# Rotary embedding in the second attention stage: rotating chunks of even and odd dimensions on VectorE instead of with a permuting matmul

## The chip, the cores and the metric

The kernel runs on one core of a Trainium2 chip. The metric is the device time of one execution in microseconds (us); lower is better. A program is compared with another by the median of several runs, and each kernel has one profiled execution besides.

## The reference

The reference chains four layers over 8 batches of 512 tokens of 256 values: causal attention with 16 heads and post-norm, a mixture of 7 experts, a second attention with rotary embedding and sigmoid weights, and a second mixture with 8 experts and a last norm. What is changed is in the second attention. Per batch, and per head of 16 dimensions:

```
q = rms_norm(x) @ q_w.T + q_b          # the same for k
x1, x2 = q[..., ::2], q[..., 1::2]     # even and odd dimensions
q_rot = stack([-x2, x1], -1).reshape(q.shape)
q = q * cos + q_rot * sin              # the same for k
scores = q @ k.T / 4
weights = sigmoid(scores) / (sum(sigmoid(scores)) + 1e-8)
```

The tables are `cos(emb)` and `sin(emb)` with `emb = [freqs, freqs]`, so the value of dimension d depends on d and the position.

## The kernel before

**Stages.** a is the first attention, b its experts, c the second attention, d its experts in blocks of 128 rows, e the last norm. Each engine (SP queues DMAs, PE, ACT, DVE, POOL) runs its own unrolled program, and semaphores tie them together.

**Passes of stage c.** `slots` emits a sequence of turns. Turn s projects batch s (transposes of x, then the q, k, v matmuls and the rotation), runs attention for batch s-1 and the output product, norm and routing for batch s-2. I call such a turn a pass. The first pass with a projection (s = 0) has no attention; seven passes (s = 1 to 7) have both. Of these s = 1 ("second") has no routing yet, s = 2 to 6 are the five "body" passes, and s = 7 ("seventh") is the last with a rotation and has no norm of a next batch. All work but attention is a list `others`, dealt out between the attention's steps by fixed weights (`COST`), so that every engine meets the steps in one order written out at build time (`spread_out`, L194).

**The attention's steps.** "st" is a unit of four score matmuls (L706) into one of two ST buffers, "av" the four matmuls with v (L724) into OT. ACT turns scores to weights (L839) in a ring of four. A unit of ST waits until the activation two units back is done. "oe" is ACT's copy of OT (L844), "on" the transpose on PE (L734) and the division on DVE (L909 to L916, which ends in `o_nat`), "oT" and "y" the output product (L742, L750), "rT" and "lg" the transposes and matmuls of the router (L760, L767).

**The projection and rotation of a chunk.** A chunk is 128 rows (16 dimensions of 8 heads) by 512 positions. Chunks 0 and 1 are q, chunks 2 and 3 are k, each for heads 0 to 7 and 8 to 15; the order is 0, 2, 1, 3. Step "qk": PE multiplies (L1462) into one of three shared PSUM banks, ACT adds the bias and copies to one of two `qk_flat` tiles (L1497), for which it waits until the rotation before last has used the tile. Step "ro": PE multiplies the copy by the constant matrix `rot` (L1468), which swaps even and odd rows and changes the sign, into another shared bank. DVE multiplies the copy by the cosines (L1586) and the bank by the sines (L1589), adds (L1594), and splits the sum in a bfloat16 part, a second (L1596 to L1598) and, on POOL, a third (L1629). SP saves the three parts of the chunk to DRAM in one DMA (L1414). Step "st_q", after the second and the fourth chunk: nine DMAs (L608, L612 in `stack_up`) read the parts back in the stacked order that the score matmuls use.

```
L245 project = [("qk", 0), ("qk", 2), ("ro", 0), ("qk", 1), ("ro", 2), ("st_q", 0), ("qk", 3), ("ro", 1),
L246            ("v", 0), ("ro", 3), ("v", 1), ("st_q", 1)]
```

**The banks.** `Banks` gives the three shared PSUM banks out in turn to the keys of `bank_keys` (L289). PE waits, before it writes a bank, until the reader of the use three before is done. In a body pass of stage c there are 24 uses, four of them by "ro".

**Other parts that the change touches.** POOL adds the output bias to x (L1635, `x_res`), once in a pass, after DVE's last row of `x_out` (L943). At the start ACT's queue loads the constants, `rot`, `cos_t` and `sin_t` last (L2050); DVE waits for all of them before its first instruction (L1050), and its first work on the first batch is L1074. The weights of stage c are scaled on DVE by four instructions (L1568). Stage d has row buffers `b_rows`, stage d's tables `t_...` and stage e's statistics in tiles of their own; `carve` takes others from the arena.

## Time and profile before

| what | value |
|---|---|
| runs of the kernel before | 1757.6, 1755.45, 1753.68 us |
| median | 1755.45 us |
| the profiled execution's own time | 1758.4 us |
| its span, from first to last instruction | 1756.7 us |
| PE busy | 1462.9 us, 83% |
| PE weight loads | 954.2 us, 54% |
| DVE busy | 926.7 us, 53% |
| ACT busy | 692.1 us, 39% |
| POOL busy | 494.1 us, 28% |
| mean granted TensorE clock | 0.893 |

In the profile "L12" is line 12 of the kernel. A row of a timeline has the start and the length of an instruction in us, its engine, line, operation, the tile it writes and those it reads, and in brackets how long its engine sat idle before it and what ended that. "x4" means four such instructions merged. A float32 matmul appears as two instructions. Names of tiles are those of the program: `scratch` is `qk_cos`, `mask` is `qk_sin` in stage c. "remote" and "unknown queue" are releases that the profile can't name. A stretch table has the busy time of each engine in a stretch of time.

### The profile page before, as it was taken

How to read it: one execution, taken by the hardware profiler on the slowest of the kernel's cores; microseconds unless marked ns; L12 is line 12 of the kernel's file. 1: busy time of each engine (PE TensorE's matmuls, PEld its weight loads, DVE VectorE, ACT ScalarE, POOL GpSimd, SP SyncE). 2: the span in 40 equal slices, each digit the busy share in tenths (PEclk: the TensorE clock that was granted, in tenths of full speed). 3: DMA queues.
4: the chain of work that ended last, by engine and by line, in shares of the span. 5: the costliest groups of instructions: out<-in, count | busy, mean ns of one | idle time of the engine just before them, and what ended most of it. 6: DMA issues, size and time to landing. Idle time of an engine off the chain costs nothing.

```text
span 1756.7 us, 31255 instructions
## 1 busy us (share of the span) xinstructions
PE 1462.9 (83%) x10303; PEld 954.2 (54%) x10304; DVE 926.7 (53%) x3456; ACT 692.1 (39%) x952; POOL 494.1 (28%) x415
## 2 busy tenths in 40 slices
PE   3688898888988828999848999999998839999992
PEld 1245454454544525666524555555555528999991
DVE  2667758777678431111164667657655353444444
ACT  1154443534434511111016566667665712222223
POOL 4022324243332521121210022321322132444442
PEclk8798888888987858999968999999999959999996
DMA  6854335254350303343134564356427243444446
GB/s 157 199 114 98 80 89 131 70 134 88 78 112 14 110 16 108 99 115 102 22 72 84 121 122 106 82 117 133 101 63 165 77 158 77 72 72 68 73 64 206
DMA packets 119182, 174.27 MB, mean 99 GB/s; under 512 B 17127, under 2 KB 101249, under 8 KB 112912
## 3 DMA queue, kind: packets, MB, share of 16 engines
q1 hardware_dynamic: 95808, 148.05, 34.4%
q0 software_dynamic: 20400, 22.37, 8.0%
q10 hardware_dynamic: 2848, 2.24, 0.4%
q8 instruction: 71, 1.16, 0.3%
q14 instruction: 55, 0.45, 0.1%
HBM read 107.18 MB, written 72.69 MB: 102 GB/s over the span
## 4 chain that ended last, share of the span: by engine, by line
PE 62%; DVE 13%; issue 7%; ACT 4%; DMA 3%; another core or an unknown queue 2%; POOL 1%; SPq 0%; DVEq 0%; POOLq 0%; ACTq 0%
PE ST L706 9%; PE OT L724 8%; PE ST L1813 7%; PE shared L1825 6%; PE ST L1264 6%; DVE scratch L1098 4%; PE OT L1272 3%; PE shared L1272 3%; PE shared L750 3%; PE shared L1462 2%; PE shared L767 2%; PE shared L798 2%; ACT arena L839 2%; PE shared L815 2%
## 5 line engine op out<-in xcount | busy, mean ns | idle before, releaser
L839 ACT ACTIVATE arena<-ST 128x1024 f32<-128x1024 f32 x416 | 414.7, 1024 | 283.8 <-PE ST L706 263.8
L1098 DVE CUSTOM_DVE_ANT_0 scratch<-shared,mask 128x512 bf16<-128x512 f32 (+3 forms) x512 | 229.1, 485 | 90.7 <-PE shared L815 73.7
L706 PE MATMUL ST<-arena 96*128 96x256 bf16 (+2 forms) x1792 | 256.0, 279 | 20.6 <-DMA arena<-qk_parts 13.5
L724 PE MATMUL OT<-arena,v_aug 128*32 128x256 f32 (+1 forms) x3584 | 255.6, 387 | 4.6 <-POOL arena L1166 2.6
L706 PEld LDWEIGHTS ST<-arena 96*128 96x128 bf16 (+1 forms) x1792 | 158.8, 102 | 123.9 <-issue 49.8
L815 PE MATMUL shared<-arena 96*128 96x512 bf16 (+3 forms) x512 | 126.8, 325 | 58.1 <-DVE mx L1098 22.6
L1920 POOL DMA_INDIRECT sum<-arena,block_to_row x71 | 111.0, 1564 | 166.8 <-DMA sum<-arena,block_to_row 115.0
L724 PEld LDWEIGHTS OT<-arena,v_aug 128*32 128x32 f32 x3584 | 85.6, 111 | 120.3 <-issue 74.1
L1166 POOL TENSOR_SCALAR_AFFINE_SELECT arena<-arena 128x512 f32<-128x512 f32 (+1 forms) x96 | 78.6, 819 | 256.6 <-ACT arena L839 256.6
L1825 PE MATMUL shared<-arena 128*128 x568 | 134.2, 379 | 0.0
L815 PEld LDWEIGHTS shared<-arena 96*128 96x128 bf16 x512 | 42.9, 103 | 139.1 <-issue 59.4
L1644 POOL DMA_INDIRECT slot_x<-x_out,row_to x64 | 63.6, 994 | 173.8 <-DVE keep L1557 156.7
L1825 PEld LDWEIGHTS shared<-arena 128*128 128x128 f32 x568 | 102.5, 190 | 11.0
L1629 POOL TENSOR_TENSOR qk_src<-qk_rest,qk_src 128x512 bf16<-128x512 f32 x32 | 38.4, 1201 | 248.5 <-DVE qk_src L1598 248.5
L1264 PE MATMUL ST<-arena 128*128 128x512 f32 x224 | 99.9, 605 | 5.1 <-ACT arena L1283 5.1
L1327 POOL DMA_INDIRECT sum<-arena,b_to x28 | 43.4, 1551 | 179.7 <-DVE arena L1310 171.3
L798 PE MATMUL shared<-xT,w_qkv 128*128 128x512 f32 x128 | 74.7, 718 | 17.3 <-DMA xT<-in_xT 14.8
L1889 DVE COPY arena<-shared 128x256 f32<-128x256 f32 x71 | 30.1, 424 | 97.6 <-PE shared L1803 72.8
L926 DVE TENSOR_TENSOR y_b<-shared,x_res 128x512 f32<-128x512 f32 x32 | 22.1, 691 | 109.5 <-issue 40.3
L1293 DVE TENSOR_SCALAR arena<-ST 128x512 f32<-128x512 f32 x28 | 19.4, 691 | 111.6 <-PE ST L1264 111.6
L1176 POOL DMA_INDIRECT slot_x<-x_out,row_to x64 | 62.6, 979 | 49.6 <-DVE row_to L975 31.8
L1870 ACT ACTIVATE arena<-ST 128x512 f32<-128x512 f32 x70 | 41.8, 597 | 85.0 <-PE ST L1813 80.3
(208 smaller groups left out, 2339.7 us busy)
## 6 DMA issues: line engine op xcount, KB each, us to landing
arena<-qk_parts SPq DMA_DIRECT2D x224, 128.0 KB, 7.1
qk_parts<-qk_src SPq DMA_DIRECT2D x64, 384.0 KB, 2.7
arena<-qk_parts SPq DMA_DIRECT2D x32, 384.0 KB, 4.4
block_rows<-slot_x SPq DMA_DIRECT2D x71, 130.0 KB
arena<-qk_parts SPq DMA_DIRECT2D x32, 256.0 KB, 5.3
sum<-x_out SPq DMA_DIRECT2D x16, 512.0 KB, 2.9
arena<-in_experts_inter SPq DMA_DIRECT2D x7, 1024.0 KB, 5.1
arena<-in_experts_out SPq DMA_DIRECT2D x7, 1024.0 KB, 9.5
```

The lines of the kernel that those rows point to most:

```text
L706: mm = pe.matmul(ST[n % 2][:, i * 256 + at:i * 256 + at + nq], K[par][0:rows, h, kb * P:(kb + 1) * P], Q[par][0:rows, h, q0:q0 + nq], star ...
L724: mm = pe.matmul(OT[32 * i:32 * i + 32, q0:q0 + nq], v_aug[par][:, kb, g * GH + i, :], PT[n % RING][:, i, at:at + nq], start=(u == 0), sto ...
L798: mm = pe.matmul(bank[:, :], w_qkv[:, c, n * P:(n + 1) * P], xT[:, c, :], start=(c == 0), stop=(c == CD - 1))
L815: mm = pe.matmul(bank[:, at:at + S - qb * P], Q[par][0:SK, head, qb * P:(qb + 1) * P], K[par][0:SK, head, qb * P:S], start=True, stop=True)
L839: act.activation(PT[n % RING][:, :, :], ST[n % 2][:, :].rearrange("p (h n) -> p h n", h=GH), func, scale=ATT_SCALE).then_inc(L["exp"], 1)
L1098: taken = dve.tensor_tensor_reduce(out=junk[n % 2][:, at:at + m], in0=bank[:, at:at + m], in1=mask[:, 0:m], scale=1.0, scalar=LOW, op0=ALU ...
L1166: pool.affine_select(out=v, in_=v, compare_op=ALU.is_ge, fill=0.0, base=0, pattern=[[0, GH], [0, blocks], [-1, P]], channel_multiplier=1). ...
L1264: mm = pe.matmul(up_banks[m % 4], wi[par][:, c, m * P:(m + 1) * P], xgT[:, c, :], start=(c == 0), stop=(c == CD - 1))
L1272: mm = pe.matmul(down_banks[t // 2][:, (t % 2) * D:(t % 2 + 1) * D], hT[:, m, t * P:(t + 1) * P], wo[par][:, m, :], start=(m == 0), stop=( ...
L1813: mm = pe.matmul(UP[par][:, f * P:(f + 1) * P], w1_now[par][:, c * F1 + f * P:c * F1 + (f + 1) * P], bxT[par][:, c * P:(c + 1) * P], start ...
L1825: mm = pe.matmul(Y_BANK[par][:, 0:D], bhT[par][:, c * P:(c + 1) * P], w2t[:, bass.ds(e * 1024 + c * D, D)], start=(c == 0), stop=(c == KF ...
L1920: pool.indirect_dma_start(out=sum1, out_offset=bass.IndirectOffsetOnAxis(ap=b_to_row[:, i:i + 1], axis=0), in_=by[i], in_offset=None, boun ...
```

## The change

Chunks are cut differently. Chunk n now holds, for eight heads, both q (rows 0 to 63) and k (rows 64 to 127), and only the even (n even) or only the odd dimensions (n odd); chunks 0 and 1 are heads 0 to 7, chunks 2 and 3 heads 8 to 15. The partner of every row of chunk n stands in the same row of chunk n ^ 1. So the rotation of chunk n is `flat[n] * cos - flat[n ^ 1] * sin` for even n and with a plus for odd n, all on DVE. The matmul, its bank, its sign matrix and the reorder of chunks go. The host lays out weights, biases and tables to match (`paired`, `rows`). In more detail:

- "ro" of an even chunk on DVE waits for both copies of the pair; there are four `qk_flat` tiles instead of two, and ACT waits only for the rotation of the batch before.
- the sine multiply reads `qk_flat` instead of a PSUM bank, and DVE waits for it in its chain (`ROPE` is 5).
- a chunk is saved by two DMAs, of 64 partitions each, the q and the k half; the count of the semaphore doubles.
- the tables have a second half each (512 KB more in sum), `rot` (64 KB) isn't loaded, and there are 13 constant loads instead of 14.
- the scaling of the weights by four instructions goes over strided columns.
- to make room, `b_rows`, `t_bf` and stage e's statistics move to the arena, and stage d's tables start at the place of `bhT` and `by`.

```diff
-        project = [("qk", 0), ("qk", 2), ("ro", 0), ("qk", 1), ("ro", 2), ("st_q", 0), ("qk", 3), ("ro", 1),
+        project = [("qk", 0), ("qk", 1), ("ro", 0), ("qk", 2), ("ro", 1), ("st_q", 0), ("qk", 3), ("ro", 2),
                    ("v", 0), ("ro", 3), ("v", 1), ("st_q", 1)]
...
-        if step in ("xT", "qk", "ro", "v", "on", "oT", "y", "rT", "lg", "ps", "mx", "mr"):
+        if step in ("xT", "qk", "v", "on", "oT", "y", "rT", "lg", "ps", "mx", "mr"):
...
-        rot = sb("rot", [P, P])
-        cos_t = sb("cos_t", [P, S])
-        sin_t = sb("sin_t", [P, S])
+        cos_t = sb("cos_t", [P, 2, S])
+        sin_t = sb("sin_t", [P, 2, S])
...
-        qk_flat = [sb(f"qk_flat{i}", [P, S]) for i in range(2)]
+        qk_flat = [sb(f"qk_flat{i}", [P, S]) for i in range(4)]
...
-        CONST_DMAS = 14
+        CONST_DMAS = 13
...
-        ROPE = 4
+        ROPE = 5
...
                     elif step == "ro":
-                        order = CHUNKS.index(n)
-                        wait(sp, L["stacked"][par][n % 2], half * STACK_DMAS)
+                        pair, odd = n // 2, n % 2
+                        wait(sp, L["stacked"][par][pair], half * STACK_DMAS)
                         settle(sp)
-                        sp.wait_ge(L["q3"], k * 4 + (order + 1))
+                        sp.wait_ge(L["q3"], k * 4 + (n + 1))
                         settle(sp)
-                        sp.dma_start(parts[par, n // 2, n % 2, :, :, :].rearrange("j p n -> p j n"),
-                                     qk_src[n][:, :, :]).then_inc(L["parts_saved"], 16)
+                        for side in range(2):
+                            sp.dma_start(parts[par, side, pair, :, odd * 64:odd * 64 + 64, :].rearrange("j p n -> p j n"),
+                                         qk_src[n][side * 64:side * 64 + 64, :, :]).then_inc(L["parts_saved"], 16)
...
-                        sp.wait_ge(L["parts_saved"], k * 64 + (32 * n + 32))
+                        sp.wait_ge(L["parts_saved"], k * 128 + (64 * n + 64))
...
-                    elif step == "ro":
-                        bank, ready = banks.acquire(pe, turn, ("ro", n))
-                        banks.read(pe, turn, ("qk", n))
-                        pe.matmul(bank[:, :], rot[:, :], qk_flat[CHUNKS.index(n) % 2][:, :],
-                                  start=True, stop=True).then_inc(ready, 1)
...
-                        wait(act, L["rope"], k * (4 * ROPE) + (ROPE * (order - 1) - 2))
-                        act.activation(qk_flat[order % 2][:, :], bank[:, :], ACT.Identity,
+                        wait(act, L["rope"], (k - 1) * (4 * ROPE) + (n // 2 * 2 + 1) * ROPE + 2)
+                        act.activation(qk_flat[n][:, :], bank[:, :], ACT.Identity,
                                        bias=b_qk[:, n:n + 1]).then_inc(free, 1)
...
-                    dve.tensor_scalar(w_qkv[:, c, side * D:(side + 1) * D], w_qkv[:, c, side * D:(side + 1) * D],
-                                      rn_scale[:, side, c:c + 1], None, ALU.mult).then_inc(s_w1s, 1)
+                    cols = w_qkv[:, c, 0:2 * D].rearrange("p (g s n) -> p g s n", s=2, n=64)[:, :, side, :]
+                    dve.tensor_scalar(cols, cols, rn_scale[:, side, c:c + 1], None, ALU.mult).then_inc(s_w1s, 1)
...
-                        order = CHUNKS.index(n)
-                        rest = qk_rest[order % 2]
-                        chain = Chain(dve, L["rope"], k * (4 * ROPE))
-                        chain.n = order * ROPE
-                        banks.read(dve, turn, ("qk", n))
-                        chain.unwaited(dve.tensor_tensor(qk_cos[:, :], qk_flat[order % 2][:, :], cos_t[:, :],
-                                                         ALU.mult))
-                        bank, free = banks.filled(dve, turn, ("ro", n))
-                        dve.tensor_tensor(qk_sin[:, :], bank[:, :], sin_t[:, :], ALU.mult).then_inc(free, 1)
-                        banks.read(dve, turn, ("ro", n))
-                        chain.join()
-                        settle(dve)
-                        wait(dve, L["q3"], k * 4 + (order - 1))
-                        chain.step(dve.tensor_tensor(rest[:, :], qk_cos[:, :], qk_sin[:, :], ALU.add))
-                        wait(dve, L["parts_saved"], k * 64)
+                        odd, rest, chain = n % 2, qk_rest[n % 2], Chain(dve, L["rope"], k * (4 * ROPE))
+                        chain.n = n * ROPE
+                        if not odd:
+                            banks.read(dve, turn, ("qk", n))
+                            banks.read(dve, turn, ("qk", n + 1))
+                        chain.unwaited(dve.tensor_tensor(qk_cos[:, :], qk_flat[n][:, :], cos_t[:, odd, :], ALU.mult))
+                        chain.step(dve.tensor_tensor(qk_sin[:, :], qk_flat[n ^ 1][:, :], sin_t[:, odd, :], ALU.mult))
+                        wait(dve, L["q3"], k * 4 + (n - 1))
+                        chain.step(dve.tensor_tensor(rest[:, :], qk_cos[:, :], qk_sin[:, :],
+                                                     ALU.add if odd else ALU.subtract))
+                        wait(dve, L["parts_saved"], k * 128)
                         chain.step(dve.tensor_copy(qk_src[n][:, 0, :], rest[:, :]))
...
-        b_rows = sb("block_rows", [P, RX, DX])
+        b_rows = carve(RX * DX).rearrange("p (i d) -> p i d", i=RX)
...
+        behind_weights = free_at[0]
         bhT = [carve(F1) for _ in range(2)]
         by = [carve(D) for _ in range(RX)]
...
+        free_at[0] = behind_weights
         t_a = carve(E1 * 32).rearrange("p (e n) -> p e n", e=E1)
...
-                (rot[:, :], a["c_rot"]), (cos_t[:, :], a["c_cos"]), (sin_t[:, :], a["c_sin"]),
+                (cos_t[:, :, :], a["c_cos"]), (sin_t[:, :, :], a["c_sin"]),
```

## Rows read from the trace of the kernel before

**Rows 1.** Busy time by stretches, one pass: PE, PEld, DVE, ACT, POOL, clock, DMA.
```profile
1109.00:1170.00 61.00, 57.83 (x508) 33.45 (x507) 39.86 (x140) 40.70 (x53) 15.36 (x14) 1.00 0.50 107
```

**Rows 2.** Line L1468, whole run: durations in ns; who waited for it.
```profile
L1468 PE MATMUL shared<-qk_flat,rot x64: 591/592/697, 902.0 to 1335.8; 128*128 128x512 f32 x64
...
  DVE mask L1589: 35.9, 19
```

**Rows 3.** Timeline of PE in one pass: start, us, engine, line.
```profile
1121.53 1.02 PE L1468 MATMUL shared<-qk_flat,rot 128*128 128x512 f32 x2
1122.49 1.07 PE L724 MATMUL OT<-arena,v_aug 128*32 128x256 f32 x16
1123.49 1.05 PE L706 MATMUL ST<-arena 96*128 96x256 bf16 x8
...
1131.34 0.60 PE L734 MATMUL shared<-ident,oT_raw 128*128 128x128 f32 x4
...
1135.38 1.02 PE L1468 MATMUL shared<-qk_flat,rot 128*128 128x512 f32 x2
1136.24 0.60 PE L706 MATMUL ST<-arena 96*128 96x256 bf16 x4
...
1140.72 1.02 PE L1468 MATMUL shared<-qk_flat,rot 128*128 128x512 f32 x2
...
1150.43 1.74 PE L767 MATMUL shared<-w_r,oT 128*128 128x12 f32 x15
```

**Rows 4.** Timeline of ACT in the same pass.
```profile
1121.48 1.96 ACT L839 ACTIVATE arena<-ST 128x1024 f32<-128x1024 f32 x2
...
1129.99 0.61 ACT L844 ACTIVATE oT_raw<-OT 128x512 f32<-128x512 f32 x1
```

**Rows 5.** Timeline of DVE in the same pass.
```profile
1130.67 0.69 DVE L1589 TENSOR_TENSOR mask<-shared,sin_t 128x512 f32<-128x512 f32 x1 [0.79 <-PE shared L1468]
...
1137.31 1.76 DVE L1594 TENSOR_TENSOR qk_rest<-scratch,mask 128x512 f32<-128x512 f32 x1 [0.17 <-DVE mask L1589]
...
1147.93 0.17 DVE L909 TENSOR_SCALAR o_sum<-shared 128x16 f32<-128x16 f32 x1 [0.54 <-PE shared L734]
...
1148.42 0.42 DVE L916 TENSOR_TENSOR o_nat<-shared,o_sum 128x256 f32<-128x256 f32 x1
```

**Rows 6.** Timeline of POOL in the same pass.
```profile
1135.84 2.68 POOL L1635 TENSOR_TENSOR x_res<-x_in,b_o 128x1024 f32<-128x1024 f32 x1 [0.62 <-DVE x_out L943]
```

**Rows 7.** Lines L1586 and L1589, whole run: ns, least, median, most.
```profile
L1586 DVE TENSOR_TENSOR scratch<-qk_flat,cos_t 128x512 f32<-128x512 f32 x32 | 25.9, 808 | 19.0 <-ACT qk_flat L1497 19.0
...
L1589 DVE TENSOR_TENSOR mask<-shared,sin_t 128x512 f32<-128x512 f32 x32 | 22.0, 688 | 36.4 <-PE shared L1468 35.9
```

**Rows 8.** Queue of SP: timeline, then line L1414 and its landing times.
```profile
1137.96 1.26 SPq L608 DMA_DIRECT2D arena<-qk_parts  x3
...
L1414 SPq DMA_DIRECT2D qk_parts<-qk_src x32: 359/376/380, 907.9 to 1341.0; - x32
...
DMA to landing us min/median/max: 2.5/2.7/9.7
```

**Rows 9.** GB/s in 40 slices of 0 to 60 us; timeline of DVE.
```profile
GB/s 0 44 134 320 391 369 308 311 132 3 0 0 0 0 262 28 234 87 218 191 164 153 142 108 258 251 33 229 175 191 158 137 130 150 363 373 329 336 336 338
...
14.27 0.28 DVE L1050 MEMSET no_row<- 128x260 f32 x1 [14.15 <-DMA sin_t<-in_c_sin]
...
17.79 0.69 DVE L1074 TENSOR_TENSOR qk_rest<-qk_flat,qk_src 128x512 f32<-128x512 f32 x1 [0.38 <-ACT qk_flat L866]
```

**Rows 10.** Timeline, first two passes of the second stage.
```profile
902.16 0.69 ACT L1497 ACTIVATE qk_flat<-shared,b_qk 128x512 f32<-128x512 f32 x1 [1.88 <-PE shared L1462]
...
903.89 0.69 DVE L1594 TENSOR_TENSOR qk_rest<-scratch,mask 128x512 f32<-128x512 f32 x1 [0.17 <-DVE mask L1589]
...
926.82 1.89 PE L706 MATMUL ST<-arena 96*128 96x256 bf16 x8 [13.53 <-DMA arena<-qk_parts]
...
985.66 1.18 PE L742 MATMUL shared<-ident,o_nat 128*128 128x128 f32 x8 [3.01 <-DVE o_nat L916]
```

More of the change, by code:

```diff
@@ L94 @@
 CHUNKS = (0, 2, 1, 3)
+ROT = (0, 1, 2, 3)
 AHEAD = {True: ("xl", "xt", "qk", "qs", "st_q"), False: ("xl", "cb")}
@@ L1626, in emit @@
                     if step == "ro":
[L1627 to L1629 removed]
+                        pool.wait_ge(L["q2"], k * 4 + (n + 1))
+                        pool.tensor_tensor(out=qk_src[n][:, 2, :], in0=qk_rest[n % 2][:, :],
                                            in1=qk_src[n][:, 1, :], op=ALU.subtract).then_inc(L["q3"], 1)
@@ L1930, in build @@
         e_rows = [e_all[:, i * EB:(i + 1) * EB, :] for i in range(N_E)]
-        e_stats = sb("e_stats", [P, NB * TB, 6])
-        e_mv = sb("e_mv", [P, NB * TB, 2])
-        e_small = sb("e_small", [P, 4, NB * TB])
+        e_stats = arena[:, 18432:18432 + NB * TB * 6].rearrange("p (t n) -> p t n", n=6)
+        e_mv = arena[:, 18688:18688 + NB * TB * 2].rearrange("p (t n) -> p t n", n=2)
+        e_small = arena[:, 18816:18816 + 4 * NB * TB].rearrange("p (n t) -> p n t", n=4)
         e_load = [sem(f"e_load{i}") for i in range(N_E)]
@@ L2097, in shape_constants @@
     emb = np.concatenate([freqs, freqs], axis=-1)
-    cos = np.repeat(np.cos(emb).astype(np.float32).T, HH, axis=0)
-    sin = np.repeat(np.sin(emb).astype(np.float32).T, HH, axis=0)
-    rot = np.zeros((P, P), np.float32)
-    for d in range(0, HD, 2):
-        for h in range(HH):
-            rot[(d + 1) * HH + h, d * HH + h] = -1.0
-            rot[d * HH + h, (d + 1) * HH + h] = 1.0
+    rows = lambda t: np.stack([np.tile(np.repeat(t[:, odd::2].T, HH, axis=0), (2, 1)) for odd in range(2)], axis=1)
+    cos, sin = rows(np.cos(emb).astype(np.float32)), rows(np.sin(emb).astype(np.float32))
     return {
         "c_ident": np.eye(P, dtype=np.float32), "c_before": np.triu(np.ones((P, P), np.float32), 1),
-        "c_mask": mask, "c_lane": lane, "c_rot": rot, "c_cos": cos, "c_sin": sin,
+        "c_mask": mask, "c_lane": lane, "c_cos": np.ascontiguousarray(cos), "c_sin": np.ascontiguousarray(sin),
     }
@@ L2118, in laid_out @@
     side = lambda w: np.stack([turned(row) for row in w])
+    paired = lambda q, k: np.stack([w.reshape(w.shape[:-1] + (2, HH, HD // 2, 2)) for w in (q, k)], axis=-5).transpose(
+        *range(q.ndim - 1), *(q.ndim - 1 + np.array([1, 4, 0, 3, 2]))).reshape(q.shape[:-1] + (2 * D,))
     return {
```

12 lines of the change are left out of this document (3 added, 9 removed).

## The prediction

> **What bounds the kernel now.** I read the busy time by stretches first. One pass of the second attention stage (the stretch between two batches) takes 60.9 us, and in it PE is busy 57.8 of 61 us, DVE 39.9, ACT 40.7, POOL 15.4, at a granted clock of 1.00, which is the 2.4 GHz level [rows 1]. So PE paces this stage, and work taken off PE is worth time until another engine is late. The second view is that of the line that disappears, L1468: 64 matmuls, two for each of 32 chunks, and DVE waited for them 19 times, 35.9 us [rows 2]. The third is the timeline of PE, ACT, DVE and POOL through one pass, to see what would be late next [rows 3 to 6]. Next come L1586 and L1589, the multiply from SBUF and the one from PSUM [rows 7], then the saves and stacks on SP [rows 8], and last the start of the program and of the stage, where PE waits and the cost of the change shows [rows 9, 10].
>
> **PE: four rotations of a pass.** From the start of an L1468 pair to the start of the next PE instruction are 0.96 us at the first (1121.53 to 1122.49) and 0.86 us at the third (1135.38 to 1136.24); I count the second and the fourth (1140.72) at 0.95 like the first [rows 3]. That is 3.7 us of PE per pass, and with seven passes that both rotate and attend, 26 us. It isn't all gained:
> - First: behind L1468 come the OT matmuls and then eight ST matmuls at 1123.49, the second four of which overwrite the buffer whose activation ends at 1121.48 + 1.96 = 1123.44 [rows 3, 4]. Those four now start at 1123.98 and can go to 1123.5: gain 0.5 us.
> - Second: L734 (1131.34) needs ACT's copy, which ran from 1129.99 to 1130.60 right behind two activations and moves up by no more than the 0.5 us above; L734 can go to about 1130.25 [rows 3, 4]. Gain 0.6 more.
> - Third and fourth: the buffers ahead are ready, so 0.86 and 0.95 in full.
> Sum at L767 (1150.43): 2.9 us per pass, if DVE keeps up.
>
> **DVE: does it keep up?** The number of its rotation instructions stays six per chunk. The second chunk no longer waits 0.79 us for L1468 at 1130.67 [rows 5]. The first now waits for both copies on ACT instead: the second of them ends about where the activations of 1121.48 start, two multiplies of 0.68 behind it end at 1122.9; so far the one sine multiply ended 0.69 behind L1468's 1122.49, at 1123.2 [rows 3, 4, 5]: 0.3. So DVE gets 1.1 us ahead. But from the first chunk to L916 DVE has hardly another gap: the wait of 0.54 us ahead of L909 is the last [rows 5]. And the sine multiply changes its source, from PSUM to SBUF. The duration alone costs nothing (median 684 against 691 ns), but L1586, with two SBUF inputs, took up to 2300 ns and L1589, with one, never over 693 [rows 7]. The addition L1594 at 1137.31, also with two SBUF inputs, took 1.76 us, beside POOL's L1635, which reads SBUF from 1135.84 to 1138.52 [rows 5, 6]. In the new kernel the third chunk's sine multiply falls on L1635, wherever DVE got ahead before: it, or the addition behind it, ends only after POOL's instruction. L1635 is itself released by DVE 1.1 us earlier (by the last row of x_out), but then the sine multiply and the addition both have to pass it, one before and one behind or both behind: begun behind DVE's two multiplies at about 1135.75, with some 2.35 us to itself, it ends at 1138.1 and the addition at 1138.8, not 1139.07: of the 1.1 us, 0.25 is left. Then L909, which DVE could have begun 0.54 us before 1147.93, comes at 1147.15 and L916 ends at 1148.05 instead of 1148.84 [rows 5]. The logits' matmuls L767 take the bank that L916 reads (three banks go round; without the rotations a body pass has 20 uses instead of 24, and this pair stays neighbours). So L767 starts at 1148.15, not 1147.53: the gain of a pass is 1150.43 - 1148.15 = 2.3 us.
> The Trainium skill, SBUF — State Buffer, section Who interferes with whom, has a rule against this change: a VectorE instruction with two SBUF inputs and a GpSimd one that reads SBUF exclude each other for a whole instruction, one with a single SBUF input does not. The trace agrees with it (2300 against 693 ns). By the rule the sum is that of 2.3 us a pass, without it 2.9.
>
> **Sum over the passes.** Five body passes at 2.3 make 11.5. The last pass with a rotation has no piece of the next batch's norm ahead of L909: 2.9. The first attention pass ends on DVE, for whose o_nat PE waited 3.01 us at 985.66 [rows 10]; there DVE's gain counts, about 2.0 us from its own waits for L1468. Together 16.4 us. Bounds: from 7 x 1.0 = 7, if DVE gives up its lead in each pass and a bit more, to 26, if all PE time counts.
>
> **What it costs elsewhere.**
> - Start. L1050 waits for the last table until 14.15 us, and L1074 has only 0.38 us of slack at 17.79. The tables grow by 512 KB and lose 64 KB; at the 369 GB/s seen around it that is 1.2 us, less the slack 0.8 [rows 9]. Bounds 0 (the extra bytes fill a gap) and 1.5.
> - First pass of the stage, without attention. PE stood 13.53 us for the stacked chunks (926.82) [rows 10], behind the chain copy, rotation, save, stack. The first chunk now needs the second copy, 902.16 + 0.69 = 902.85; two multiplies behind it put the sum at 904.3 instead of 903.89 [rows 10]: 0.4. Each save is two DMAs of 64 partitions, so SP issues one more (0.36 to 0.38 us each) and the second half lands that much later: 0.4. Bounds for this pass 0.4 and 3, if the second half takes the 2.5 us of the shortest landing on top [rows 8].
> - In the other passes these 32 extra issues cost nothing: the first stacks are issued at 1137.96, the pass that reads them begins at 1170, and a save lands within 9.7 us [rows 8]. They hide behind the attention of the batch before; with that cover gone each would cost what the first pass pays.
> - ACT no longer waits for the rotation before it overwrites a copy: bounds 0 and some tenths of gain. The four multiplies of the weights are strided and lie where DVE idles. The tiles moved into the arena are written and read by the same stages as before, with no wait added: nothing, bounds -0.3 and +0.5.
> Total: 16.4 - 0.8 - 0.8 = 14.8 us. The profiled execution has a span of 1756.7 us (its own time 1758.4), so 1741.9; the three runs have a median of 1755.45, 3 us under that execution's time, and the forecast is made on the median: **1740.6 us**.
>
> **The rivals.**
> - A: all of it. If ACT and DVE slide along with PE (activations are idle before most units), 26.1 us less 1.6: 1731. For it: PE busy 57.8 of 61. Against: the two places above where an activation or L844 ends on the same tenth. A half-way form, 2.9 us in every pass, gives 1737.
> - B: the gain is eaten. The waits of DVE for PE go, and POOL's come; with 0.3 us or less per pass, and the 1.6 us of costs, the time is within 0.2% (3.5 us, about what a measurement of this kernel can tell from no change). For it: DVE's gapless stretch. Against: DVE's L916 ends 1.59 us ahead of L767 now [rows 3, 5].
> - C: slower. Each sine multiply meets POOL and is held as long as the worst L1586: 2300 - 684 = 1.6 us [rows 7]. Four are 6.5 us, less the 1.1 of waits gone: DVE is 5.4 us late, L916 ends at 1154.2, L767 starts behind it, and each pass is 3.8 us longer. Seven passes and 1.6: 1755.45 + 28 = 1784. It decides from 1.6 us of DVE lateness per pass on. Against: POOL's subtraction of a chunk starts behind that chunk's last cast, so only the next chunk's first multiply stands beside it, and DVE has other work in between for two of four. For it: the worst L1586 shows that such a hold happens today.
> That the change doesn't do what it says is excluded by the code: no rotation matmul is left to issue.
>
> **How the numbers follow.** The forecast as worked out 0.58, A with its half-way form 0.28, B 0.08, C 0.06. The forecast's own terms span 1735 to 1747; A reaches to 1731 and a step towards B to 1749. I take 1730 to 1749 and leave C and most of B out. Chances: faster 0.87, within 0.2% 0.07, slower 0.06.
>
> **What would show it.** Right: no 64 matmuls from the qk_flat tiles; PE still busy over 93% of a pass; passes 58.6 us apart; the new sine multiply with a mean over 0.8 us and single ones over 1.7 beside L1635; a wait of PE for DVE's o_nat of some tenths ahead of L767; the first attention matmuls of the stage some 0.8 us later against the stage's start; L1050 about 1.2 us later. Wrong: passes of 57.2 us (A), of 60.6 (B), or longer than 60.9 with PE waiting for DVE (C). A granted clock below 1.00 in the passes would be a cause that this sum does not have.

## The result, and the profile after

The changed kernel takes **1739.31 us** (median of 4 runs, 1737.22 to 1745.83), the kernel before, beside it, 1756.53 (4 runs). The ratio is 0.9897, 95% interval 0.987 to 0.9925: 18.1 us faster, where 14.8 were forecast (the two medians are 17.2 us apart). In the second comparison below the ratio is 0.9924 (0.9898 to 0.995), 13 us. Ratios and intervals are those on record, estimated from the runs; the quotient of two medians differs from them by up to 0.2%. The forecast of the time holds. The step on which its largest term rests, the cap by DVE, does not, and the number came out in part by luck.

The profiled execution of after is its slowest run (1745.83 us); that of before took 1758.4 us (span 1756.7), 3 us more than the median. So a difference of spans is not that of the medians. First the page, with the busy time of PE and DVE and the granted clock, then three windows, each one body pass long (us, PE, PEld, DVE, ACT and POOL busy, clock, DMA share, GB/s); compare [rows 1]:

```profile
span 1744.3 us, 31137 instructions
PE 1442.9 (83%) x10239; PEld 945.9 (54%) x10240; DVE 930.4 (53%) x3456; ACT 690.9 (40%) x952; POOL 495.6 (28%) x415
PEclk8789888888888858999967999999998959999996
```
```profile
1045.00:1104.00 59.00, 56.49 (x500) 33.92 (x499) 40.70 (x140) 41.15 (x53) 16.12 (x14) 0.96 0.52 112
1104.00:1163.00 59.00, 56.44 (x498) 33.96 (x497) 40.69 (x140) 40.78 (x52) 15.59 (x15) 0.96 0.53 110
1221.00:1279.00 58.00, 55.45 (x502) 33.15 (x501) 40.67 (x140) 40.77 (x54) 15.17 (x14) 0.99 0.54 115
```

The 64 matmuls of [rows 2] are gone (10303 to 10239), and PE is still busy 96% of a pass. But the granted clock of a pass is 0.96 to 0.99, where the pass of [rows 1] had 1.00. The prediction had named this as a cause that its sum does not have.

Where the time lies is read from milestones on PE: the first transposes of the stage, the first attention matmul, and the o_nat transposes L742 that close each pass. Of the kernel before (its other two are in [rows 10]):

```profile
893.09 1.94 PE L1455 MATMUL shared<-ident,xn 128*128 128x128 f32 x8 [21.62 <-DVE small L1377]
...
1290.20 1.90 PE L742 MATMUL shared<-ident,o_nat 128*128 128x128 f32 x8 [1.17 <-DVE o_nat L916]
...
1355.26 1.94 PE L742 MATMUL shared<-ident,o_nat 128*128 128x128 f32 x8 [1.16 <-DVE o_nat L916]
...
1406.25 1.90 PE L742 MATMUL shared<-ident,o_nat 128*128 128x128 f32 x8 [1.16 <-DVE o_nat L916]
```

The same of after:

```profile
893.58 1.94 PE L1456 MATMUL shared<-ident,xn 128*128 128x128 f32 x8 [21.55 <-DVE small L1377]
...
929.09 1.89 PE L706 MATMUL ST<-arena 96*128 96x256 bf16 x8 [19.59 <-DMA arena<-qk_parts]
...
984.59 1.94 PE L742 MATMUL shared<-ident,o_nat 128*128 128x128 f32 x8 [2.34 <-DVE o_nat L916]
...
1277.83 1.06 PE L742 MATMUL shared<-ident,o_nat 128*128 128x128 f32 x8 [1.32 <-DVE o_nat L916]
...
1341.24 1.94 PE L742 MATMUL shared<-ident,o_nat 128*128 128x128 f32 x8 [1.46 <-DVE o_nat L916]
...
1395.52 1.06 PE L742 MATMUL shared<-ident,o_nat 128*128 128x128 f32 x8 [1.16 <-DVE o_nat L916]
```

By stretch, before and after: up to the stage 893.1 and 893.6 (0.5 lost); first projection 33.7 and 35.5 (1.8 lost); first attention pass 58.8 and 55.5 (3.3 gained); five body passes from 985.66 or 984.59 on, 304.5 and 293.2 (11.3 gained, 2.26 each); the seventh 65.1 and 63.4 (1.7 gained); the eighth 51.0 and 54.3 (**3.3 lost**); the rest 350.5 and 348.8 (1.7 gained). Sum: 12.4 us, the difference of the spans.

Now the places where the forecast put its cap. The lines of DVE in after (name, shapes, count, busy us, mean ns, idle before), for [rows 7]; then the third chunk's sine multiply beside POOL's sum, and o_nat and the logits behind them, on DVE, POOL and PE:

```profile
L1582 DVE TENSOR_TENSOR mask<-qk_flat,sin_t 128x512 f32<-128x512 f32 x32 | 34.6, 1082 | 0.0
L1581 DVE TENSOR_TENSOR scratch<-qk_flat,cos_t 128x512 f32<-128x512 f32 x32 | 24.4, 761 | 35.2 <-ACT qk_flat L1492 35.2
L1584 DVE TENSOR_TENSOR qk_rest<-scratch,mask 128x512 f32<-128x512 f32 x32 | 22.1, 692 | 1.1
```
```profile
1130.02 2.86 DVE L1582 TENSOR_TENSOR mask<-qk_flat,sin_t 128x512 f32<-128x512 f32 x1
...
1142.19 0.42 DVE L916 TENSOR_TENSOR o_nat<-shared,o_sum 128x256 f32<-128x256 f32 x1
```
```profile
1129.56 2.78 POOL L1625 TENSOR_TENSOR x_res<-x_in,b_o 128x1024 f32<-128x1024 f32 x1 [0.61 <-DVE x_out L943]
```
```profile
1142.41 0.61 PE L706 MATMUL ST<-arena 96*128 96x256 bf16 x4
1142.86 1.85 PE L767 MATMUL shared<-w_r,oT 128*128 128x12 f32 x16
```

The sine multiply's mean rose from 688 to 1082 ns, with single ones of 2.86 us that end half a us behind POOL's L1625. The additions, at a mean of 865 ns in the same view of before, came down to 692. So the hold of the forecast is there. Yet L767 follows L706 with no wait: DVE's L916 ends at 1142.61, a quarter of a us ahead. Only one sign of DVE stands on PE's side, in the view of who waited for the read of v (L1596):

```profile
L1596 DVE SCALAR_TENSOR_TENSOR v_aug<-shared,small,b_v x32: 472/476/484, 916.1 to 1326.4; 128x256 f32<-128x256 f32 x32
...
  PEld shared L760: 2.1, 5
```

0.4 us in each of five passes, beside other work of PE. What is new is at the end of a pass, on PE:

```profile
1156.04 2.28 PE L724 MATMUL OT<-arena,v_aug 128*32 128x256 f32 x32
1159.12 0.63 PE L734 MATMUL shared<-ident,oT_raw 128*128 128x128 f32 x4 [0.81 <-ACT oT_raw L844]
1161.07 1.94 PE L742 MATMUL shared<-ident,o_nat 128*128 128x128 f32 x8 [1.32 <-DVE o_nat L916]
1162.81 1.85 PE L1456 MATMUL shared<-ident,xn 128*128 128x128 f32 x8
1164.49 0.60 PE L706 MATMUL ST<-arena 96*128 96x256 bf16 x4
```

PE waits 0.81 us for ACT and 1.32 us for DVE, and the sixteen transposes behind run at the 1.2 GHz level: 3.42 us from L742 to L706, where a pass that keeps 2.4 GHz takes 1.81 (e7, at 1095.38).

One more thing stands at the start of a pass, on ACT, in some profiles and not in others. The first chunk's copy to `qk_flat`, in before, in e7 and in e10:

```profile
1118.52 0.69 ACT L1497 ACTIVATE qk_flat<-shared,b_qk 128x512 f32<-128x512 f32 x1 [4.71 <-remote]
```
```profile
1106.10 0.69 ACT L1492 ACTIVATE qk_flat<-shared,b_qk 128x512 f32<-128x512 f32 x1 [3.27 <-remote]
```
```profile
1028.55 0.69 ACT L1492 ACTIVATE qk_flat<-shared,b_qk 128x512 f32<-128x512 f32 x1 [2.42 <-PE shared L1463]
```

These passes all start at full clock. The copy begins 10.9, 10.7 and 8.1 us behind the pass's L742. In the third ACT waits for PE's result and takes it at once. In the first two it stands idle until something that the profile can't name ("remote"); I call this "ACT is held". PE's next scores then wait for ACT, 1.0 us in the pass of before and 1.1 in that of e7, against 0.2 in e10. Over the whole execution ACT has 18 to 44 us of such idle time in each profile of before, of after and of e1 to e8, and none in e9 to e12. What holds it is not shown.

### The profile page after: what moved, and what is told of

The parts are those of the page before. It is cut to its first block, busy times and chain, and to the rows that moved or that the text cites. A ratio compares the mean times of both kernels' runs of the same rounds, so it can differ in the third digit from the quotient of the medians.

```text
span 1744.3 us, 31137 instructions
## 1 busy us (share of the span) xinstructions
PE 1442.9 (83%) x10239; PEld 945.9 (54%) x10240; DVE 930.4 (53%) x3456; ACT 690.9 (40%) x952; POOL 495.6 (28%) x415
## 3 DMA queue, kind: packets, MB, share of 16 engines
q8 instruction: 70, 1.15, 0.3%
## 4 chain that ended last, share of the span: by engine, by line
PE 60%; DVE 14%; issue 7%; ACT 5%; DMA 4%; POOL 1%; another core or an unknown queue 1%; SPq 0%; DVEq 0%; POOLq 0%; ACTq 0%
PE ST L706 8%; PE OT L724 7%; PE ST L1805 7%; PE shared L1817 6%; PE ST L1264 6%; DVE scratch L1098 4%; PE shared L750 3%; PE shared L1463 3%; ACT arena L839 3%; PE OT L1272 3%; PE shared L1272 3%; PE shared L767 2%; PE shared L798 2%; PE shared L815 2%; PE shared L742 2%
## 5 line engine op out<-in xcount | busy, mean ns | idle before, releaser
L706 PE MATMUL ST<-arena 96*128 96x256 bf16 (+2 forms) x1792 | 257.4, 279 | 26.7 <-DMA arena<-qk_parts 19.6
L706 PEld LDWEIGHTS ST<-arena 96*128 96x128 bf16 (+1 forms) x1792 | 157.4, 102 | 128.3 <-issue 45.5
```

The source lines that it names most:

```text
L706: mm = pe.matmul(ST[n % 2][:, i * 256 + at:i * 256 + at + nq], K[par][0:rows, h, kb * P:(kb + 1) * P], Q[par][0:rows, h, q0:q0 + nq], star ...
```

## The experiments

My theories after this reading were CLOCK (PE is given back over 3 us a pass, and loses part of it to the low clock at the pass ends), DVE-CAP (the forecast) and PE-ONLY. The twelve runs are in four groups (e1 to e4, e5 to e8, e9 to e11, e12), each beside before on the same chip. The first two groups have the same chip number on record, the third and the fourth one each of their own. Times are compared as ratios; the chips of the last two groups ran before in 1738 to 1739 us, the first two groups in 1754 to 1756. "Body pass" is the mean of five, from the first and the sixth L742 of the profile.

```
                            ratio to before (95%)     body pass  eighth
after                       0.9897 (0.9870-0.9925)      58.65     54.3
e1 matmuls in the gaps      0.9912 (0.9884-0.9939)      57.79     55.5
e2 xn transposes first      0.9863 (0.9835-0.9891)      57.88     53.2
e3 the same on before       0.9968 (0.9951-0.9986)      59.62     51.5
e4 rotation's matmul back   1.0041 (1.0021-1.0060)      61.47     51.4
e5 after again              0.9924 (0.9898-0.9950)      58.10     55.0
e6 one more DVE multiply    1.0134 (1.0106-1.0162)      64.37     55.8
e7 x + b_o later            0.9936 (0.9913-0.9959)      57.84     54.2
e8 before, split saves      1.0011 (0.9996-1.0026)      60.82     51.0
e9 e6 and e7 together       0.9972 (0.9958-0.9986)      58.29     52.4
e10 first pass without POOL 0.9927 (0.9909-0.9945)      58.00     51.9
e11 combined                0.9876 (0.9853-0.9899)      56.98*    51.8
e12 weights later           0.9931 (0.9910-0.9952)      58.64     52.7
```
(*e11: the last four of the five, each 56.98; before: 60.91 and 51.0.)

**e1: matmuls that keep PE busy in the gaps.**
```diff
+ if (step, n) == ("on", NG - 1):
+     pe.matmul(ST[0][:, 0:512], ident[:, :], cos_t[:, 0, :], start=True, stop=True)
  attention_pe(pe, L, banks, False, turn, step, n, U1)
+ if (step, n) == ("on", NG - 1):
+     pe.matmul(ST[0][:, 0:512], ident[:, :], cos_t[:, 0, :], start=True, stop=True)
+     pe.matmul(ST[0][:, 512:768], ident[:, :], cos_t[:, 0, 0:256], start=True, stop=True)
```


> After, plus matmuls of constants in TensorE's two gaps at every pass end (one of 512 columns ahead of the last o transposes, 512 + 256 columns behind them; 8 times in the kernel). They compute nothing. Theory CLOCK (the change gives PE back over 4 us a pass, and some 2 us of it are lost again because the transposes of a pass's end run at 1.2 GHz after the gaps): L742 x8 back from 1.6-1.9 us to about 1.1, L1456 x8 from 1.85 to about 1.1, passes from 58.8 to about 57, the whole 9 to 12 us faster than after (about 1728). Theory DVE-CAP (my forecast: VectorE's held sine multiply sets the pass): the clock may rise but passes stay within 0.3 us of 58.8 and the time within 3 us of after. Theory PE-ONLY without a clock effect: 0 to +2 us.

All eight L742 groups ran in 1.06 or 1.07 us, as CLOCK had it, and the clock of two passes (1092.6 to 1209.0) was 1.00. The time did not follow: 0.9912, between the two ratios of after. The added matmuls (2.8 us at each pass end, for gaps of 2.1) are not the reason: the first body pass takes 56.90 us, beside 56.80 for a pass of e7 that starts at full clock without them. The second takes 57.59, the last three 58.1 to 58.2, and in these three ACT is held, for 2.6 to 2.7 and then 3.3 us. PE's waits (engine, line, releaser: us in total, times, longest), for two such passes of e1 and then for two of after (1104 to 1221.4):

```profile
PE ST L706 <- ACT arena L839: 2.2, 6, 0.6
```
```profile
PE ST L706 <- ACT arena L839: 0.4, 2, 0.2
```

A PE that starts these passes at full clock waits 0.9 us more a pass for the held ACT. So CLOCK's 9 to 12 us fall for the time in this group. Its mechanism does not: in the pass without a hold a start at full clock pays (e10, below, has both kinds in one execution).

**e2 and e3: real work in the gap.** On after, and the same on before:
```diff
-            start += turn_x
+            start = turn_x + start
```


> After, with the transposes of xn (L1456) moved ahead of those of o_nat (L742) at six pass starts: real work in the gap that waits for o_nat. CLOCK: the 1.3 us gap closes and the rest of the transposes run at 2.4 GHz: 1.3 + 1.5 = 2.8 us a pass, six times, 15 to 17 us faster than after (about 1723). DVE-CAP: the freed PE time turns into a wait at L767 or L760 for DVE; less than 4 us. PE-ONLY: only the gap, 6 x 1.2 = 7 us.

> The kernel before with the same step moved. There the transposes already run at 2.4 GHz, so all theories give the gap alone: 6 x 1.1 = 6 to 7 us faster than before (about 1749). What it tells: if it gains as much as e2 does against after, then e2's gain isn't the clock; CLOCK wants e2 to gain at least 6 us more than e3 does.

e3 gives 0.3% (5.6 us), the gap alone, as all theories had it. e2 gives 0.3 to 0.6% against the two ratios of after, 6 to 11 us. CLOCK wanted 15 to 17, and 6 more than e3, and PE-ONLY's 7 us fit better; each interval is about 5 us to either side, and ACT is held in some of e2's passes too, so this is not a clean test of CLOCK.

**e4: the matmul back, read by nobody.**
```diff
+                        pe.matmul(bank[:, :], ident[:, :], cos_t[:, 0, :], start=True, stop=True)
                         for c in range(CD):
                             mm = pe.matmul(bank[:, :], w_qkv[:, c, n * P:(n + 1) * P], xT[:, c, :],
```


> After, with one matmul of the rotation's size (128x512, constants) put back ahead of each of the 32 chunk projections, into the bank that the projection then overwrites. No reader waits for it. CLOCK and PE-ONLY: 4 x 0.86 = 3.4 us of PE a pass; PE-ONLY wants all of it, +22 to +27 us against after (about 1764). CLOCK wants the same less what the clock gives back where the gaps are no longer reached cold, +12 to +24. DVE-CAP: PE had 0.5 to 1.4 us a pass of slack against DVE, so +13 to +20.

1.17 to 1.44% over after, 20.5 to 25 us for 32 matmuls, and the body pass 2.8 to 3.4 us longer. Of the 3.4 us of PE a pass, nearly all counts, so PE sets these passes: DVE-CAP's 13 to 20 us lie below what was measured. PE-ONLY (22 to 27) and CLOCK (12 to 24) are not told apart. The matmul stands ahead of a chunk's projection, not where the rotation's stood.

**e5: after again**, the baseline of the second group.

> The changed kernel itself, as the baseline of this chip for the next three. All theories: 1737 to 1742 us, passes 58.6 to 58.8.

Its median is 1743.92 us where before has 1754.03, 2 us above the expected interval. The body pass is 58.10, below the expected one: two of its five began at full clock, and the first, of 59.58 us in after, takes 58.20.

**e6: one more multiply on DVE.**
```diff
                         chain.unwaited(dve.tensor_tensor(qk_cos[:, :], qk_flat[n][:, :], cos_t[:, odd, :], ALU.mult))
+                        chain.step(dve.tensor_tensor(qk_sin[:, :], qk_flat[n][:, :], cos_t[:, odd, :], ALU.mult))
```


> After, with one more VectorE multiply of 128x512 (two SBUF inputs, 0.69 us, overwritten by the sine multiply behind it) in each of the 32 chunks: 2.8 us of VectorE a pass. DVE-CAP (my forecast): VectorE sets the pass from v's read to o_nat's, so most of the 2.8 us shows, passes 60.5 to 61.5, +12 to +17 us. PE-ONLY and CLOCK: VectorE had over 1 us of slack ahead of L1520 and more ahead of L926, so passes stay within 0.4 us of 58.7; some +1 to +3 us come from the first pass alone, where VectorE is on the path (4 x 0.7 at most).

A miss of every theory: 1777.8 us beside e5's 1743.92, 34 us, for 2.8 us of DVE a pass. The view of who waited for v's read has the reason, and two neighbouring passes the size:

```profile
  PE shared L760: 11.7, 5
```
```profile
1157.00 0.66 PE L760 MATMUL shared<-ident,x_out 128*128 128x128 f32 x4 [2.35 <-DVE v_aug L1597]
...
1158.80 1.96 PE L767 MATMUL shared<-w_r,oT 128*128 128x12 f32 x16
...
1218.10 1.12 PE L760 MATMUL shared<-ident,x_out 128*128 128x128 f32 x4 [2.35 <-DVE v_aug L1597]
...
1220.98 3.43 PE L767 MATMUL shared<-w_r,oT 128*128 128x12 f32 x16
```
```profile
1116.30:1177.00 60.70, 54.97 (x496) 31.80 (x496) 43.36 (x144) 40.21 (x52) 15.15 (x14) 1.00 0.51 108
1177.00:1242.50 65.50, 60.65 (x496) 36.32 (x497) 43.37 (x144) 40.65 (x52) 15.24 (x14) 0.90 0.48 100
```

The same wait of 2.35 us stands in both. In the first pass PE keeps 2.4 GHz behind it, and from L760 to the next L742 (1177.07) are 20.1 us. In the second it runs at 1.2 GHz for about 10 us, L767 takes 3.43 instead of 1.96, and the same stretch (to 1242.53) takes 24.4. PE is busy 5.7 us longer in this pass, for the same 496 matmuls (its transposes, too, were at the lower level). Four of the five passes are of this kind, 64.6 to 65.8 us. So DVE has next to no margin ahead of L760, and a wait inside a pass costs up to three times its length (2.35 us of wait and 4.4 us of slower work).

**e7: POOL's sum later.**
```diff
-    save = ([("xs", 3), ("sv", 3)] if route else []) + ([("xp", 0)] if attn else [])
+    save = ([("xs", 3), ("sv", 3)] if route else []) + ([("xp", 0)] if attn and not (route and prep and not causal) else [])
...
-                      + project[6:] + mixed(combine, rows + route_1 + route_2 + route_3) + scatter)
+                      + project[6:10] + ([("xp", 0)] if attn else []) + project[10:] + mixed(combine, rows + route_1 + route_2 + route_3) + scatter)
```


> After, with POOL's x + b_o (L1625) moved from beside the third chunk's sine multiply to behind the fourth chunk's third part. DVE-CAP: the held multiply (2.86 us) goes back to 0.7 and the pass gains 0.6 to 0.9 us, 3 to 5 us in all. PE-ONLY and CLOCK: L1582's maximum falls or moves to another instruction of VectorE, passes stay within 0.2 us, the time within 1 us of after.

The maximum of L1582 falls from 2862 to 1650 ns, PE's wait for v is gone, and the time stays (0.9936 against 0.9924; 1743.93 against 1743.92 us). In after the hold lies just inside DVE's slack.

**e8: split saves on before.**
```diff
-                        sp.dma_start(parts[par, n // 2, n % 2, :, :, :].rearrange("j p n -> p j n"),
-                                     qk_src[n][:, :, :]).then_inc(L["parts_saved"], 16)
+                        for side in range(2):
+                            sp.dma_start(parts[par, n // 2, n % 2, :, side * 64:side * 64 + 64, :].rearrange("j p n -> p j n"),
+                                         qk_src[n][side * 64:side * 64 + 64, :, :]).then_inc(L["parts_saved"], 16)
```


> The kernel before with each chunk's save split in two of 64 partitions, as the change has it, and nothing else. My forecast's term: +0.4 us in the first pass, nothing in the passes behind it: 0 to +1 us. If the split makes the transfers collide with other work: first attention matmul of the stage over 1 us later, or passes over 61.2.

1.0011 (0.9996 to 1.0026): nothing that can be measured. The first attention matmul comes 33.85 us behind the stage's first transposes (888.23 to 922.08), 0.1 more than in before. The term of 0.4 is 0.1.

**e9: e6's multiply with e7's order.**

> e6 (one more VectorE multiply a chunk) with POOL's x + b_o moved as in e7. In e6 PE waited 2.35 us for v_aug at L760 in a pass, and in a pass where that wait was followed by a low clock the matmuls behind it took twice their time. Theory PORT HOLD (the held multiply, 2.85 us instead of 0.69, is what uses up VectorE's margin): the move takes 2.2 us out of VectorE's queue ahead of v's read, the wait at L760 all but goes and with it the fall of the clock: passes 58 to 60, 1745 to 1755 us. Rival (VectorE's own work sets it, the hold is absorbed): passes stay above 62, the time above 1768.

```profile
1123.23 0.66 PE L760 MATMUL shared<-ident,x_out 128*128 128x128 f32 x4 [0.18 <-DVE v_aug L1597]
```

PORT HOLD: the wait is 0.18 instead of 2.35, the 2.2 us by which the held multiply is shorter (2.84 to 0.68). The ratio is 0.9972 instead of 1.0134, body passes 58.29 instead of 64.37. The chips differ, so the two ratios are less sure than the wait, which is read in the profiles. The same 2.8 us of DVE work a pass cost a body pass 0.55 us once POOL's sum is not beside it (57.35 in the two passes that start at full clock, 56.80 in such passes of e7 and e10 without a hold); most of the rest is in the first two passes, where DVE is on the path (the wait ahead of the first L742 is 5.19 us). The Trainium skill, SBUF — State Buffer, section Who interferes with whom, has this as an exclusive lock between a VectorE instruction with two SBUF inputs and a GpSimd one that reads SBUF; the held instructions of 2.84 and 2.86 us agree.

**e10: the first pass without POOL.** In that pass alone DVE makes the third part (and POOL skips it):
```diff
                         dve.tensor_copy(qk_src[n][:, 1, :], rest[:, :]).then_inc(L["q2"], 1)
+                        if turn.kind == "first":
+                            dve.wait_ge(L["q2"], k * 4 + (n + 1))
+                            dve.tensor_tensor(qk_src[n][:, 2, :], rest[:, :], qk_src[n][:, 1, :],
+                                              ALU.subtract).then_inc(L["q3"], 1)
```


> After, with the third part of the four chunks of the stage's first pass made by VectorE instead of POOL (that pass alone), so that no POOL instruction of two SBUF inputs lies beside the sine multiplies there. Theory HOLD IN THE FIRST PASS: no sine multiply over 0.8 us near 907 to 913 us, and the first attention matmul (L706) comes 33.2 to 34.3 us behind the stage's first transposes (35.5 and 34.8 in the two profiles of after, 33.7 in before). Rival (the split saves or the second copy set it): still 34.8 or more. The whole time within 2 us of after, below what these rounds can tell.

```profile
873.93 1.94 PE L1456 MATMUL shared<-ident,xn 128*128 128x128 f32 x8 [21.61 <-DVE small L1377]
...
906.86 1.89 PE L706 MATMUL ST<-arena 96*128 96x256 bf16 x8 [18.09 <-DMA arena<-qk_parts]
```

32.9 us, less than expected and less than before's 33.7. In after, the second chunk's sine multiply had stood beside the first one's third part on POOL, and the third chunk's (1.64 us) beside the second one's:

```profile
907.65 1.65 DVE L1582 TENSOR_TENSOR mask<-qk_flat,sin_t 128x512 f32<-128x512 f32 x1
```
```profile
907.29 1.46 POOL L1619 TENSOR_TENSOR qk_src<-qk_rest,qk_src 128x512 bf16<-128x512 f32 x1 [29.37 <-DVE qk_src L1589]
```

In e10 all four take 0.68 or 0.69. But 32.9 is not the price of the holds alone. DVE makes the third part in 0.69 us where POOL took 1.15 to 1.53, and in e10 DVE's first multiply comes 8.8 us behind the first transposes, in after 9.9. e7 has both holds and its first multiply at 8.7, and reaches 34.3: inside the range expected of e10.

What e10 shows besides is the price of the clock. Here ACT is never held, and the L742 of its second, third and fourth body pass are:

```profile
1020.49 1.06 PE L742 MATMUL shared<-ident,o_nat 128*128 128x128 f32 x8 [1.27 <-DVE o_nat L916]
```
```profile
1077.29 1.50 PE L742 MATMUL shared<-ident,o_nat 128*128 128x128 f32 x8 [1.27 <-DVE o_nat L916]
...
1135.72 1.89 PE L742 MATMUL shared<-ident,o_nat 128*128 128x128 f32 x8 [1.27 <-DVE o_nat L916]
```

The pass that starts at full clock takes 56.80 us, the next, which starts at the low clock, 58.43, and the waits inside the two are the same. Up to its first chunk (L1463) the slow one needs 1.63 us more, so all that the low clock takes is lost.

**e11: combined.** e2's order, e7's, e10's first pass, and the copies of oT on DVE:
```diff
-                    elif step == "oT":
-                        copy_bank(act, banks, turn, ("oT", n), oT[:, n, :])
...
+                    elif step == "oT":
+                        bank, free = banks.filled(dve, turn, ("oT", n))
+                        dve.tensor_copy(oT[:, n, :], bank[:, :]).then_inc(free, 1)
```


> After, with e2's order (transposes of xn ahead of those of o_nat), e7's (x + b_o later), e10's first pass, and the two copies of oT (L848, ACT) done by VectorE, which is idle there. If a pass is PE's work and the waits of its first matmuls for ACT (L706 and L750 for L839 and L848, 1.0 us in e2) and the gap ahead of the o_nat transposes: passes 56 to 57, 8 to 14 us faster than after (1727 to 1732). If something else holds a pass at 57.9 (VectorE, which gets 1.4 us a pass more): passes 57.5 or more, the time within 4 us of e2's.

1715.73 us beside 1722.91 of e10 (after but for its first pass) on the same chip: 7.2 us faster, and the intervals of the two ratios don't meet. Body passes are 56.98 with a clock of 1.00:

```profile
1081.00:1139.00 58.00, 55.23 (x499) 32.65 (x500) 40.07 (x143) 40.33 (x51) 15.62 (x14) 1.00 0.54 115
```

This version is faster than both kernels. The 8 to 14 us expected were just missed. Between the profiles of e10 and e11 the five body passes gain 4.1 us and the seventh pass 1.9, and the first projection and the first attention pass lose 1.3. e10's own pass at full clock took 56.80, so in a body pass the gain is that the last four of the five start at full clock, not that such a pass is shorter. Which of the edits does it is not separated: by the ratios e2's order alone, on another chip, is as fast (0.9863).

**e12: stage d's weights later.** The load ("wl", 0) stands behind the routing of the eighth pass instead of ahead of it.

> After, with the load of stage d's first eight weight blocks (8 x 512 KB on SP, issued from 1333.7 us on, before the eighth pass begins) moved behind that pass's routing. In both profiles of after on the first two chips the eighth pass took 54.3 and 55.0 us against 51.0 in before, with PE and ACT idle together (1.5 to 3.3 us, issue and remote) and low clock behind it, while these loads kept the DMA engines above 90%. Theory LOADS (an instruction fetch waits behind the loads): no such gap in the new place of the pass's start, the eighth pass 50.5 to 52 us, the time 2 to 4 us below after, unless the gap moves with the loads. Rival (the gap has nothing to do with the loads, or the routing behind which they now run is hit instead): the eighth pass 53.5 us or more, the time within 2 us of after. On a chip where after has no gap (e10: 51.9) the time stays as it is.

The eighth pass of after, which lost 3.3 us, had this on PE; ACT waited 3.33 us, until 1349.34, in the same moment (releaser "remote"):

```profile
1347.72 1.07 PE L724 MATMUL OT<-arena,v_aug 128*32 128x256 f32 x16
1350.42 0.61 PE L706 MATMUL ST<-arena 96*128 96x256 bf16 x4 [1.63 <-issue]
1351.88 0.77 PE L706 MATMUL ST<-arena 96*128 96x256 bf16 x4 [0.85 <-ACT arena L839]
1352.45 3.45 PE L750 MATMUL shared<-w_o,oT 128*128 128x256 f32 x8
```

In e12 the gap isn't there (52.7 us), but neither is it in e10, with the load in its old place on a chip of the same speed, and the ratio is the same (0.9931 and 0.9927). In the second attention stage of e9 to e12 neither PE nor ACT has such idle time, so e12 could not remove it. In e10 the loads fill the DMA engines as they do in after (share 1.05 from 1308 to 1325, 1.03 from 1333.7 to 1352), without a gap. So the loads alone don't make it; whether they have a part is open.

## Why the prediction was right, step by step

**The sum of a body pass (2.3 us)** came out at 2.26 in the profiled execution and 2.7 in the second group (60.82 in e8, 58.10 in e5). Its mechanism was wrong in the last link. The working had DVE hold L767 behind L916, which would cut 2.9 to 2.3; L767 did not wait. Take the pass of [rows 3], which begins at 1107.65 with full clock and ACT held, and one of e5 with the same start:

```profile
1107.65 1.06 PE L742 MATMUL shared<-ident,o_nat 128*128 128x128 f32 x8 [1.16 <-DVE o_nat L916]
```
```profile
1214.00 1.06 PE L742 MATMUL shared<-ident,o_nat 128*128 128x128 f32 x8 [1.27 <-DVE o_nat L916]
...
1253.87 1.85 PE L767 MATMUL shared<-w_r,oT 128*128 128x12 f32 x16
```
```profile
1253.20 0.42 DVE L916 TENSOR_TENSOR o_nat<-shared,o_sum 128x256 f32<-128x256 f32 x1
```

In e5 L767 comes 39.87 us behind L742, just where the working has it without DVE (1147.53 less 1107.65 is 39.88). L916 ends 39.62 behind L742, where the working had 40.40. The hold itself happened where the step put it, but DVE had got further ahead: POOL's sum, which DVE releases, began 1.6 us earlier than in before (26.57 against 28.19 us behind L742 [rows 6]), not 1.1. So the hold ended in DVE's remaining slack. e7 shows that it costs nothing there, e6 with e9 that the slack was less than one more multiply a chunk.

**What took the cap's place is how a pass starts.** The body passes of before and e8, and of the five kernels with after's work on PE (after, e5, e7, e10, e12), by the time from L742 to the first L706 and by ACT (us, number of passes):

```
start of the pass               before's side          after's side
full clock (1.8), ACT held      60.73 to 60.88 (5)     58.03 to 58.09 (4)
full clock, held less or not    60.25 (1)              57.66, 56.80, 56.80
low clock (2.7 to 3.4)          60.88 to 61.11 (4)     58.07 to 58.59 (16), 59.58, 59.61
```

In the first row a pass gains 2.8 us, in the last 2.7 (without the two longest): that is the 2.9 of the working without the cap, with its first two terms (0.5 and 0.6) limited by ACT as they stand there. The 2.26 of the profiled execution compares unlike passes: four of before's five are of the first row, all of after's of the last. So two errors of about the same size met, a cap of 0.6 that did not come and starts at low clock that the sum did not have. This part of the hit is luck. Why more passes start low after the change (18 of 25 against 4 of 10) is not shown; from the second body pass on, the wait ahead of L742 is 1.27 to 1.32 us on after's side and 1.16 or 1.17 on before's.

**What the low clock costs depends on ACT.** Where ACT is held, a pass at full clock waits for it and is hardly shorter (58.06 against 58.20 to 58.34 in e5 and e7). Where it is not, the whole 1.6 us show (e10; in e9 57.35 against 58.80 to 59.07). No pass on before's side starts at full clock with ACT free, so the gain under these conditions is not known.

**The other terms.** First attention pass: 2.0 forecast, 3.3 measured from the first attention matmul on; DVE paces it, as said, and e6 lengthens the wait ahead of its L742 from 2.33 to 5.19 us. Seventh pass: 2.9 forecast, 1.7 measured. The eighth was costed at nothing and lost 3.3, the unexplained gap above; with no gap it takes 51.9 (e10). Start: 0.8 forecast; L1050 came 0.64 us later (its wait is 14.79 us), the stage 0.5. First pass: 0.8 forecast (0.4 the second copy, 0.4 the saves), 1.8 measured, 1.0 in e5. The saves are 0.1 (e8), the second copy is 0.4 as worked out (the first addition begins 11.2 instead of 10.8 us behind the first transposes). What the working missed are two holds, 1.65 and 1.64 instead of 0.69 us at the sine multiplies of the second and the third chunk. With them the last third part is done 1.7 us later than in before. Rival C had said that only the next chunk's first multiply would stand beside POOL's subtraction; that one slips in ahead of it (907.05), and the sine multiply behind is held.

**The rivals.** A with its half-way form had 0.28. Its 2.9 us a pass are nearer the 2.7 to 2.8 of equal starts than the cap's 2.3, and the median of 1739.3 lies between its 1737 and the forecast. It names the mechanism better than the forecast did. B and C didn't come, but C's mechanism is real: in e6 DVE passes its margin, and the kernel is 1.3% slower than before. I had set C's turning point at 1.6 us of lateness; e6, with 2.8 us more on DVE, made PE wait 2.35, so it lies near 0.4, and the clock makes the price steeper than C's sum had it. Of the signs named, the passes of 58.6 us, PE's busy share, the sine multiply's mean and singles came, and so did the clock below 1.00; the wait for o_nat ahead of L767 did not, and the two delays of the start were 1.8 us for 0.8 and 0.64 for 1.2.

## What to carry to other kernels

When work comes off the engine that sets the pace, look at the margin of the next engine at every point where the two meet, not only at the last: here it was 0.25 us at one and none at another, and one more instruction a chunk would have turned the gain of 1% into a loss. Before adding work to VectorE, move POOL's reads of SBUF away from its instructions with two SBUF inputs. Price a wait of PE by what runs behind it at the lower clock, but check whether the next engine would have made PE wait there anyway. And before reading a gain from the mean of a few passes, sort the passes by how they start: here that moved it from 2.3 to 2.8 us.

## What the runs showed of the hardware that was not expected

- A wait of PE of 2.35 us in the middle of a pass is followed in some passes by 2.4 GHz and in others by about 10 us at 1.2 GHz, in the same kernel and execution: 60.7 against 65.5 us a pass (e6). Three of the four long passes began with L742 in 1.94 us, but one of them (1242.53) and the short one with 1.06, so the clock at the pass's start doesn't decide it. What does isn't settled.
- What a start at the low clock costs depends on the next engine: 1.6 us a pass where ACT is free (e10, 58.43 against 56.80), 0.1 to 0.3 where it is held (e5 and e7).
- ACT can stand still for 2.6 to 4.7 us with no releaser that the profile names, at the same place of many passes. In the eighth pass of after PE stands still with it, 1.6 us. ACT's idle time of this kind is 18 to 44 us in each profile of before, of after and of e1 to e8, and zero in e9 to e12, whose chips run the kernel before 1% faster (1738 and 1739 against 1754 to 1757 us). Whether the one makes the other is not shown.
